# Attention rows gathered by indirect DMA and turned by DMA transposes in blocks 1 to 7, with the two halves added on GpSimd

## The reference, cut to what matters

```python
def _feature_map(x, gamma, beta):
    return _layer_norm(x * gamma + beta)
q = _feature_map(q, gamma, beta)
k = _feature_map(k, gamma, beta)
q = q * D ** (-0.5)
attn = jnp.einsum('bqhd,bkhd->bhqk', q, k) ** 2
attn = jnp.where(mask, attn, 0.0)
o = jnp.einsum('bhqk,bkhd->bqhd', attn, v)
z = jnp.sum(attn, axis=-1)
o = o / (jnp.swapaxes(z, 1, 2)[..., None] + EPS)
...
h = _L0_tok_ref(x, ...)
h = h + _L0_attn_ref(_layernorm(h, axis=-1), ...)
h = h + _L0_ffn_ref(_layernorm(h, axis=-1), ...)
```

## Time and profile before

| What | us |
|---|---|
| timed runs, median of 3 | 1402.48 (1400.31 to 1403.24) |
| profiled execution, its own time | 1400.2 |
| its span in the profile | 1398.4 |
| PE busy | 1306.7 (93%) |
| DVE, ACT, POOL busy | 532.3, 398.7, 422.9 |
| chain that ended last | PE 83%, DVE 6%, DMA 4%, ACT 4% |

### The profile page before, as it was taken

How to read it: one execution, slowest core, us unless ns; L and a number is a source line. 1 busy time by engine, 2 the same in 40 slices (tenths; PEclk the granted TensorE clock), 3 DMA queues, 4 the chain that set the end, 5 groups by cost and what they waited for, 6 DMA issues and landing times.

```text
span 1398.4 us, 19203 instructions
## 1 busy us (share of the span) xinstructions
PE 1306.7 (93%) x7481; PEld 643.6 (46%) x7481; DVE 532.3 (38%) x1049; ACT 398.7 (29%) x703; POOL 422.9 (30%) x371
## 2 busy tenths in 40 slices
PE   5575598989999999999999999999999999999999
PEld 3352255554444444444444444444444444444444
DVE  1655567654422253226222432234222523251110
ACT  4453463440233113321233023311322123211220
POOL 0342143332144313432244213421433124321210
PEclk9888699999999999999999999999999999999999
DMA  8911100002100130003000210012001300020000
GB/s 297 288 27 23 24 1 9 8 8 54 53 8 9 31 75 8 15 15 80 19 16 8 68 38 8 15 42 64 8 8 23 83 8 15 15 68 23 0 0 30
DMA packets 101681, 55.73 MB, mean 40 GB/s; under 512 B 74180, under 2 KB 90872, under 8 KB 101112
## 3 DMA queue, kind: packets, MB, share of 16 engines
q1 hardware_dynamic: 98112, 45.77, 12.8%
q0 software_dynamic: 2560, 8.39, 2.0%
q10 hardware_dynamic: 952, 0.75, 0.2%
HBM read 29.47 MB, written 8.65 MB: 27 GB/s over the span
## 4 chain that ended last, share of the span: by engine, by line
PE 83%; DVE 6%; DMA 4%; ACT 4%; issue 2%; POOL 1%; SPq 0%; DVEq 0%; ACTq 0%
PE bank L1078 24%; PE bank L1079 24%; PE bank L1080 23%; DMA prod<-sg 3%; PE bank L1231 3%; PE bank L1073 2%; PE bank L1216 2%; PE bank L1215 2%; PE bank L1121 1%; DMA hid<-in_L_tok_norm_weight 1%; PE bank L1240 1%; ACT xT L855 1%; DVE wgu L477 1%; PE bank L1071 1%; ACT wgu L855 1%
## 5 line engine op out<-in xcount | busy, mean ns | idle before, releaser
L1078 PE MATMUL bank<-xT,wgu 128*128 128x512 f16 x1024 | 389.3, 380 | 1.4 <-DVE xT L708 1.4
L1079 PE MATMUL bank<-xT,wgu 128*128 128x512 f16 x1024 | 389.3, 380 | 0.0
L1080 PE MATMUL bank<-xT,wgu 128*128 128x512 f16 x1024 | 389.2, 380 | 0.0
L398 POOL TENSOR_TENSOR hid<-a,hid 128x512 f16<-128x512 f32 x128 | 147.9, 1156 | 512.0 <-ACT hid L855 512.0
L743 DVE SCALAR_TENSOR_TENSOR a<-bank,kap,sg 128x512 f32<-128x512 f32 x128 | 96.0, 750 | 477.5 <-PE bank L1080 324.4
L1078 PE MATMUL bank<-wd,hid 128*128 128x512 f16 x512 | 194.3, 379 | 0.0
L1079 PE MATMUL bank<-wd,hid 128*128 128x512 f16 x512 | 194.1, 379 | 0.0
L1080 PE MATMUL bank<-wd,hid 128*128 128x512 f16 x512 | 194.0, 379 | 0.0
L358 POOL TENSOR_TENSOR p<-prod,p 128x512 f16<-128x512 f32 x128 | 153.2, 1199 | 128.4 <-ACT p L855 128.4
L855 ACT ACTIVATE hid<-a 128x512 f16<-128x512 f32 x128 | 80.6, 630 | 279.5 <-DVE a L743 279.5
L1080 PEld LDWEIGHTS bank<-xT,wgu 128*128 128x128 f16 x1024 | 100.4, 98 | 121.6 <-issue 1.4
(11 more groups left out here) (178 smaller groups left out, 1245.8 us busy)
## 6 DMA issues: line engine op xcount, KB each, us to landing
out<-a SPq DMA_DIRECT2D x24, 256.0 KB, 2.2
wgu<-in_L_ffn_W_gate SPq DMA_DIRECT2D x16, 256.0 KB, 5.5
wgu<-in_L_ffn_W_up SPq DMA_DIRECT2D x16, 256.0 KB, 5.0
wd<-in_L_ffn_W_down SPq DMA_DIRECT2D x4, 1024.0 KB, 9.4
ids_b<-in_x SPq DMA_DIRECT2D x8, 256.0 KB, 3.5
out<-h_row SPq DMA_DIRECT2D x8, 256.0 KB, 2.0
xT<-in_L_tok_proj_weight SPq DMA_DIRECT2D x1, 1024.0 KB, 8.6
p<-in_L_attn_Wq SPq DMA_DIRECT2D x1, 1024.0 KB, 13.8
```

The costliest lines, as they stand in the source:

```text
L398: nc.gpsimd.tensor_tensor(hid[:, 1, s, :], a32[:, :], hid[:, 0, s, :], ALU.subtract)\
L1078: mm(dst, w[0], v[0], start=first, stop=False)
L1079: mm(dst, w[0], v[1], start=False, stop=False)
L1080: return mm(dst, w[1], v[0], start=False, stop=final)
```

## The change

For blocks 1 to 7 the lookups on TensorE go. `att` is stored once, after it is made, into four tables in HBM, one for each quad (`att_tables`, a row of 2 x 4 x 128 f16 for each id). For each quad and each 128 tokens GpSimd issues an indirect DMA that gathers the tokens' rows (2 KB each) into a staging buffer, and SP issues a DMA transpose that turns the 128 x 1024 tile into both halves of the four heads (`p_turn`). GpSimd adds the two halves into `prod` (`halves_sum`), and VectorE multiplies `prod` by `cnt` in place. There are two buffers for a quad (`PB`): `p16`, and the storage of `att`, which is free after block 0. Staging: quad 0 of the next block goes through `ids_b`, one tile after the other; quads 1 to 3 through four buffers in the last four tiles of `hid`, which ScalarE fills only from slot 12 on, after a wait for the three turns of each. The gathers stand in the slots of `FETCH_AT` (quads 1 to 3) and `NEXT_AT` (quad 0 of the next block). ScalarE no longer waits for the sums of a quad before it writes the next `p`, except in block 0; `onehotT`'s storage now holds the other one-hot tile (`onehot`). GpSimd's loop over passes is written out.

```diff
+FETCH_AT = {0: ((1, 0), (1, 1)), 1: ((1, 2), (1, 3)), 3: ((2, 0), (2, 1)), 4: ((2, 2), (2, 3)),
+            7: ((3, 0), (3, 1)), 8: ((3, 2), (3, 3))}
+NEXT_AT = (12, 14, 18, 25)
...
+            def store_tables():
+                sp.wait_ge(S["a_lo"], 4)
+                for q in range(QUADS):
+                    nc.sync.dma_start(att_tables[q].rearrange("t (l h v) -> t l h v", l=2, v=P),
+                                      att[:, :, 4 * q:4 * q + 4, :]).then_inc(S["tab_stored"], 16)
...
+            def p_turn(n, q, m):
+                way, g = fetched(n, q, m)
+                sp.wait_ge(S[f"pg_land{way}"], 16 * g + 16)
+                if n == 1 and q == 0 and m == 0:
+                    sp.wait_ge(S["tab_stored"], 64)
+                    sp.wait_ge(S["picked"], H)
+                if m == 0 and (n, q) != (1, 0):
+                    sp.wait_ge(S["heads_ready"], QUADS * n + q - 1)
+                nc.sync.dma_start_transpose(PB[q % 2][:, :, :, m * P:(m + 1) * P].rearrange("p l j t -> p (l j) t"),
+                                            stages[way]).then_inc(S[f"pt_land{way}"], 16)
...
+            def halves_sum(n, s):
+                if s < H:
+                    raw = PB[s // 4 % 2]
+                    if s % 4 == 0:
+                        for m in range(4) if s else (3,):
+                            way, g = fetched(n, s // 4, m)
+                            pool.wait_ge(S[f"pt_land{way}"], 16 * g + 16)
+                    if s < 2:
+                        pool.wait_ge(S["xm_done"], 4 * n)
+                        pool.wait_ge(S["xhada_ready"], 4 * n)
+                    nc.gpsimd.tensor_tensor(prod[:, s % 2, :], raw[:, 0, s % 4, :], raw[:, 1, s % 4, :], ALU.add)\
+                        .then_inc(S["ps_done"], 1)
...
+                nc.gpsimd.indirect_dma_start(stages[way], None, att_tables[q],
+                                             bass.IndirectOffsetOnAxis(ids_p[:, m:m + 1].bitcast(U32), axis=0))\
+                    .then_inc(S[f"pg_land{way}"], 16)
...
-            with pool.Fori(1, NB - 1) as b:
+            for b in range(1, NB - 1):
                 for s in range(SLOTS):
+                    fetch(b + 1, s)
+                    if s == 0:
+                        halves_sum(b + 1, 0)
                     pair(b, s)
+                    halves_sum(b + 1, s + 1)
...
+                        dve.wait_ge(S["ps_done"], i - H + 1)
+                        nc.vector.tensor_tensor(prod[:, s % 2, :], prod[:, s % 2, :], cnt[:, :], ALU.mult)\
+                            .then_inc(S["p_done"], 1)
...
-                for h in (0, 1) if s == 0 else (s + 1,) if s + 1 < H else ():
-                    i = H * n + h
+                for h in () if not zero else (0, 1) if s == 0 else (s + 1,) if s + 1 < H else ():
```

More of the change, by code:

```diff
@@ L96, in tower @@
         h_table = nc.dram_tensor("h_table", [VOCAB, D], F32, kind="Internal").ap()
+        att_tables = [nc.dram_tensor(f"att_table{q}", [VOCAB, 8 * P], F16, kind="Internal").ap() for q in range(QUADS)]
         wgu = sb("wgu", [P, GROUPS, DC, 2, 512], F16)
@@ L289, in block_io @@
                     if turning is not None:
+                        for m in range(4):
+                            if q < 3:
+                                p_turn(turning, q + 1, m)
+                            elif turning < NB - 1 and m < 2:
+                                p_turn(turning + 1, 0, m)
+                        if q == 2 and turning < NB - 1:
+                            load_gather_ids(turning + 1)
                         o_turn(turning, q)
+                if turning is not None and turning < NB - 1:
+                    p_turn(turning + 1, 0, 2)
                 if turning is not None:
@@ L306, in block_io @@
                         x_turn(turning, m + 1)
-            load_ids_rows(1)
+            load_gather_ids(1)
+            store_tables()
             for q in range(QUADS):
+                if q == 3:
+                    for m in range(2):
+                        p_turn(1, 0, m)
                 o_turn(0, q)
+            p_turn(1, 0, 2)
             for m in range(4):
+                if m == 3:
+                    p_turn(1, 0, 3)
                 x_turn(0, m)
@@ L402, in _ @@
                 product(0, s)
+                if s in NEXT_AT:
+                    gather(1, 0, NEXT_AT.index(s))
                 attend(0, s)
@@ L996, in feed_high @@
                 if s < FT:
+                    if s == FT - 4 and not (isinstance(b, int) and b == NB - 1):
+                        for way in range(1, 5):
+                            act.wait_ge(S[f"pt_land{way}"], 48 * (b + 1))
                     act.wait_ge(S["a_done"], FT * b + s + 1)
@@ L1195, in attend @@
             def attend(n, s):
+                zero = isinstance(n, int) and n == 0
+                tokens = onehot0 if zero else onehot
                 if s == 0:
```

100 lines of the change are left out of this document (69 added, 31 removed).

## The result

| What | before, us | after, us |
|---|---|---|
| timed runs beside each other, median (4 each) | 1402.62 (1400.31 to 1403.24) | 1476.49 (1473.39 to 1478.34) |
| profiled execution, its span | 1398.4 | 1475.0 |
| first feed-forward matmul (end of the start) | 162.75 | 170.45 |
| pass 0, from there to the finish of block 0 | 209.9 | 215.9 |
| six passes and the last feed-forward alone | 1022.4 | 1085.4 |

The account below looks back on a forecast made before the run. TensorE, busy 148.36 of 149.00 us, was taken to bound a steady pass. 1400.2 + 41 (six passes) + 2 (first pass) + 5 (start) = 1448, forecast as 1450 us on timed runs; range 1408 to 1486.

Parts of the forecast that it names:

- the ring: Steady passes: wait cycle a, hid high, hid low, halves, product, p, silu, a takes 5.80 us a slot against TensorE's 5.18.
- the forecast's own case: Whole kernel: slower with the addition cycle at 5.80 us a slot, 1435 to 1470 us; chance 0.50.
- by the gathers: Rival, GpSimd in steady passes: each gather costs 0.5 us more, giving 1480 us; chance 0.12.
- I cost the gathers at nothing: GpSimd's slots with gathers: a pair takes 2.5 us, hidden by the wait for product, p and silu, no slack left.
- by the port: Rival, steady passes: a gather shuts out VectorE's two-SBUF-input product for 1.06 us in eight slots, giving 1500 us; chance 0.05.
- Transfers nothing: Gather and transpose landings, 3.4 and 3.1 us after issue, cost nothing, being due over 10 us after issue.
- The removal's worth: TensorE, blocks 1 to 7: dropped lookups are 6.9 us per pass, 48.3 us in all, if TensorE stayed the bound.
- One steady pass: Each steady pass: last sum 5.4 us later plus 1.5 us of clock loss, 6.9 us longer; six passes 41 us.
- Pass 0: First pass, block 0 with block 1's attention: +2 us, from -5 to +9.
- hidden later on: First pass: product and eviction come about 1.1 us later in slots 2 to 7, and are hidden in later slots.
- The start: Before the first feed-forward matmul: +1.4 us in slot 14 and +3.5 at block 0's end, together +5 (0 to 7).
- Small gaps leave the clock alone: TensorE in steady passes: gaps of 0.6 us a slot were taken not to lower the clock.

Follow-up runs that it names:

- e3_no_fetch: Changed kernel with gathers and their turns run for block 1 only, blocks 2 to 7 reusing the rows in the buffers; 1462.72 us, ratio 1.043 to the kernel before.
- e1_sum_first: Changed kernel with GpSimd, in steady passes, adding the next head's halves ahead of the low half of hid; 1398.38 us, ratio 0.997 to the kernel before.
- e5_cnt_bank: On top of e1_sum_first, counts of blocks 1 to 7 copied into a PSUM bank that VectorE's product reads; 1382.86 us, ratio 0.986 to the kernel before.
- e4_no_lookup: The kernel before with the lookups of blocks 1 to 7 left out and nothing in their place; 1363.37 us, ratio 0.972 to the kernel before.
- e8_fill: Changed kernel with 24 additional matmuls into an unused bank before the last sum of each steady pass; 1465.51 us, ratio 1.045 to the kernel before.
- e10_vector_adds: On top of e9_best, VectorE instead of GpSimd adds the halves of block 1's heads in pass 0; 1365.24 us, ratio 0.973 to the kernel before.
- e6_start_p0: Changed kernel with the fourth gather's turn issued behind the last x turn, and GpSimd's halves first in pass 0's slots; 1471.94 us, ratio 1.050.
- e7_pe_unroll: On top of e1_sum_first, TensorE's loop over the six steady passes written out, without a jump back; 1387.74 us, ratio 0.990 to the kernel before.
- e9_best: e5_cnt_bank plus TensorE's loop written out and both edits of e6_start_p0; 1370.33 us, ratio 0.977 to the kernel before.

## Why the prediction came out as it did

The direction and the mechanism, the ring, were right. The time was 26 us short: 1450 forecast, 1476.5 measured, inside the range but above the forecast's own case (1435 to 1470) and near the 1480 of the rival "by the gathers", whose price was there in part (2.7 of its 5 us a pass) and for another reason. All three terms of the sum, passes, pass 0 and start, came out too small, and that the range still held is owed to its width on that side. Point by point:

**The ring** is right within 0.04: 5.76 us for the 5.80 of the sum. The addition of two f16 tiles into f32, which no row showed, takes 1.15 (estimated 1.15). The Trainium skill's page "GPSIMD Engine Reference" (section "Elementwise — side-by-side cycle accounting"), by which I had an estimate of 1.11, agrees with that row within 4%; its measurement is one of fp32 tiles, and that the type doesn't matter is what the row adds. A turn with a sum takes 7.07 (7.10) where no pair of gathers is in it, as in e3_no_fetch, and 7.33 in the two of a pass where one is. e1_sum_first shows that it is this ring that costs the time.

**"I cost the gathers at nothing"** failed, in the way that the text had left as a risk: no slack. The pair was put at 2.5 us behind the addition's 1.11 (to `a` + 6.2) and takes 2.87 (890.37 + 1.11 to 894.35, `a` + 6.58); the low half of p comes after it, and the low half of `hid` is 0.46 late: this is the sign that the prediction had named for being wrong (`hid` low behind a gather). The first of a pair takes 1.42 instead of 0.95 because the new product reads two tiles from SBUF at that moment, and not by the tests of semaphores that the rival had in mind. My rival "by the port" had the gather shut out the product; it is the product that slows the gather (e5_cnt_bank). Measured by leaving them out: 2.7 us a pass.

**"Transfers nothing"** holds in the passes as far as the waits show: by the page of the profile, gathers land 3.6 us after issue and turns 3.3 to 3.4, and TensorE's list of waits has none for them; its waits for the turns of x are 4.7 us in six passes (3.6 before).

**The removal's worth** was put at 6.9 us a pass. e4_no_lookup shows 5.4, because a gap of 1.6 us at the loop's head appears with the lookups gone. No view of the kernel before holds it, so I had no term for it at all. In the changed kernel it shifts the whole ring, since `a`(0) starts the ring.

**One steady pass.** Predicted was a last sum 5.4 us later and 1.5 behind it. In the pass from 866.36 to 1026.76 the last sum starts 102.40 us after the first matmul (968.76 less 866.36), before 93.73 (915.25 less 821.52): 8.7 later. The first matmul and `a`(0) of the pass before, and `a`(0) of this one:

```profile
821.52 0.38 PE L1078 MATMUL bank<-xT,wgu 128*128 128x512 f16 x1
...
826.97 0.75 DVE L743 SCALAR_TENSOR_TENSOR a<-bank,kap,sg 128x512 f32<-128x512 f32 x1 [2.95 <-PE bank L1080]
...
873.34 0.75 DVE L848 SCALAR_TENSOR_TENSOR a<-bank,kap,sg 128x512 f32<-128x512 f32 x1 [5.13 <-PE bank L1189]
```

Against the steps of the prediction 1.5 come from the gap at the head (`a`(0) at +6.98 instead of +5.45), 0.3 between `a`(0) and `a`(1), and 1.4 from the gathers in the fourteen turns (86.5 instead of 85.1). Behind the sum 2.3 are lost instead of 1.5; e8_fill puts what the clock takes at 2.1. Idle before the sum is 6.1 us, as predicted (about 6). In sum 10.95 in this pass instead of 6.9. Over six passes that is the larger part of the miss: 63 instead of 41.

**Pass 0**: +6.0 measured, +2 predicted (from -5 to +9). The step "hidden later on" failed: the additions were stretched as read from the earlier trace rows, but GpSimd's instructions in turn held up VectorE's on TensorE's path, a tiny one for 3.7 us by the reading above; taking the additions off GpSimd gave back 3.6 us (e10_vector_adds). And the "less 6.9" of that sum was 4.2 when only the lookups went (e4_no_lookup), so the rest of the change cost 10.2 us there.

**The start**: +7.7 measured, +5 predicted (0 to 7). The order on SP is what I described: the chain goes over the fourth gather and its turn to the last turn of x, which starts at 164.28 here and at 157.16 before:

```profile
157.18 0.51 POOL h L385
...
159.00 3.92 DMA ids_b<-att_table,ids_p
...
162.94 1.24 SPq L297
...
164.28 3.68 DMA prod<-sg
...
170.45 0.61 PE bank L1187
```

From GpSimd's instruction at 157.18 to the first feed-forward matmul it takes 13.3 us, before 8.6 (154.12 to 162.75): 4.6 for the 3.5 of the prediction. e6_start_p0 gets 3.8 of them back (9.4 from 156.64). The other 3.1, ahead of that instruction, can't be put down to the change with confidence: the same instruction stands at 154.13 in e7_pe_unroll and at 158.71 in e1_sum_first, whose programs are the same up to there.

**"Small gaps leave the clock alone"** is right for the time, not for the clock. In this pass TensorE is busy 2.27 us from 918 to 922, with a wait of 1.73 before the third sum over a quad, and in the next stretch the granted clock falls:

```profile
922.00:926.00 4.00, 4.00 (x16) 1.46 (x13) 1.83 (x5) 1.60 (x3) 3.52 (x4) 0.57 0.21 57
```

The turn of the ring beside it (`a` at 924.82 to 932.15) takes 7.33 us, like the one from 899.75 to 907.08, where the clock is 1.00. TensorE isn't what that stretch waits for, and the price comes only behind the last sum.

## What to carry to other kernels

Before a step moves to another engine, close the loop on paper: follow the moved step's result back to where the same engine waits next, and add the rows up; a ring just above the bound's time per slot (5.76 against 5.18 us) costs more than all the work that was saved, and the cure here was an order (e1_sum_first, 78 us). A step that "just fits" has to be costed with what it will run beside: two SBUF operands on VectorE beside GpSimd cost 15 us in e1_sum_first, and one operand in PSUM took that away (e5_cnt_bank). What an edit can give is measured cheaply by leaving the old work out (e4_no_lookup), and that was 20% below the sum of its instructions. It is no bound, though: with the loop written out, the passes of e9_best are shorter still (983.1 us against 990.1).

## What the runs showed of the hardware

- TensorE lost 1.6 us a pass behind a loop's jump back, after six matmuls of the body, with two or three instruction packets on their queue; with the loop written out it was gone, and a pass 1.4 us shorter. The kernel with lookups in the body had no such gap, also where three packets fell around its jump; why is open.
- A VectorE instruction on 128x8 elements lasted 3.72 us instead of 0.16, to the end of three GpSimd instructions on 128x512 that began 0.3 us later (another one of 128x8 wasn't held); a product of 128x512 with two SBUF inputs lasted 2.74 instead of 0.69, to 0.55 behind the end of two GpSimd subtractions, of which the second had begun after it.
- A gather's issue on GpSimd takes 0.95 us, and 1.42 beside a VectorE product with two SBUF inputs; with one of them in PSUM the mean of 72 is 0.96, where it was 1.05 with nothing else changed.
- Around the end of 6.1 idle us (at 968.76) the granted clock was 0.60 and 0.54 in two stretches of 4 us, 966 to 974, and 1.00 behind them; the price, by a kernel that fills the idle time with matmuls, was 2.1 us. It also fell to 0.57 behind 4 us with 2.27 busy, at no price that the trace shows.
